# Row-blocked score matmuls in the exponential pass of a two-layer attention kernel

## The reference

```python
q, k, v = split_heads(x @ wq), split_heads(x @ wk), split_heads(x @ wv)   # 16 heads of 8
scores = jnp.einsum('bhqd,bhkd->bhqk', q, k)
scores = jnp.where(causal, scores, -jnp.inf)
attn = jax.nn.softmax(scores / np.sqrt(HEAD_DIM), axis=-1)
ctx = jnp.einsum('bhqk,bhkd->bhqd', attn, v)
```

## Time and profile before

| what | value |
|---|---|
| median of 3 runs | 1313.72 us (1313.71 to 1315.61) |
| span of the profiled execution | 1311.0 us |
| TensorE busy | 1194.1 us, 91% |
| VectorE busy | 1044.4 us, 80% |
| ScalarE busy | 723.5 us, 55% |
| mean granted TensorE clock | 0.975 of full speed |
| first attention layer, about | 200 to 643 us of the span |
| second attention layer, about | 846 to 1280 us of the span |

### The profile page before, as it was taken

One profiled execution on the slowest core, in us unless ns is written; L12 is line 12 of the kernel. 1 busy time (PEld: TensorE's weight loads), 2 busy tenths in 40 slices (PEclk: granted clock), 3 DMA queues, 4 the chain that ended last, 5 costly groups with the idle time before them and its releaser, 6 DMA issues.

```text
span 1311.0 us, 21446 instructions
## 1 busy us (share of the span) xinstructions
PE 1194.1 (91%) x7781; PEld 510.1 (39%) x7781; DVE 1044.4 (80%) x3015; ACT 723.5 (55%) x861; POOL 66.6 (5%) x64
## 2 busy tenths in 40 slices
PE   1999958999999999999699979599999999999997
PEld 1455533333333333334455537233333333333336
DVE  8976588999999887875447567799999989878764
ACT  1322115566777777777332224156667777777773
POOL 5111010000000000000101000100000000000000
PEclk9999979999999999999799989799999999999999
DMA  4100142000000000000000000510000000000001
GB/s 147 34 1 1 39 131 58 2 1 2 2 1 1 2 1 2 1 1 2 1 0 1 1 1 25 154 48 2 2 1 2 2 1 1 2 1 2 2 2 33
DMA packets 23510, 23.26 MB, mean 18 GB/s; under 512 B 3134, under 2 KB 21220, under 8 KB 23404
## 3 DMA queue, kind: packets, MB, share of 16 engines
q1 hardware_dynamic: 22252, 18.73, 4.9%
q0 software_dynamic: 1152, 3.15, 0.9%
HBM read 13.20 MB, written 8.39 MB: 16 GB/s over the span
## 4 chain that ended last, share of the span: by engine, by line
PE 70%; DVE 22%; issue 4%; ACT 2%; DMA 1%; SPq 0%; DVEq 0%; ACTq 0%
PE psum L1184 18%; PE psum L1204 17%; PE psum L1164 14%; PE psum L442 9%; DVE part_max L1314 8%; PE psum L466 2%; PE psum L903 2%; PE psum L1171 2%; DVE junk L1320 2%; DVE xn L167 1%; DVE norm_v L150 1%; PE psum L1224 1%; PE psum L918 1%; DVE norm_stats L141 1%; PE psum L427 1%
## 5 line engine op out<-in xcount | busy, mean ns | idle before, releaser
L1275 ACT ACTIVATE hidden<-psum,exp_scale 128x1024 f32<-128x1024 f32 (+3 forms) x640 | 597.7, 984 | 258.9 <-PE psum L1164 137.3
L1314 DVE TENSOR_REDUCE part_max<-psum 128x1 f32<-128x512 f32 x768 | 492.1, 686 | 59.1 <-PE psum L1204 53.9
L1204 PE MATMUL psum<-k_slots,q_slots 128*128 128x512 f16 (+3 forms) x1280 | 401.2, 356 | 34.2 <-DVE part_max L1314 12.2
L1164 PE MATMUL psum<-q_slots,k_slots 128*128 128x512 f16 (+3 forms) x1280 | 330.9, 348 | 6.3 <-ACT hidden L1275 3.5
L1184 PE MATMUL psum<-hidden,v_aug 128*9 128x512 f32 (+3 forms) x2560 | 293.7, 531 | 0.1
L1320 DVE CUSTOM_DVE_ANT_0 junk<-psum,causal_add 128x384 bf16<-128x384 f32 (+3 forms) x512 | 230.6, 488 | 49.0 <-PE psum L1204 45.9
L1204 PEld LDWEIGHTS psum<-k_slots,q_slots 128*128 128x128 f16 x1280 | 114.5, 97 | 361.1 <-DVE part_max L1314 177.5
L442 PE MATMUL psum<-parts,w_parts 128*128 128x512 f16 x768 | 180.4, 387 | 1.9 <-DVE parts L843 1.9
L1164 PEld LDWEIGHTS psum<-q_slots,k_slots 128*128 128x128 f16 x1280 | 118.3, 98 | 97.8 <-ACT hidden L1275 13.9
L442 PEld LDWEIGHTS psum<-parts,w_parts 128*128 128x128 f16 x768 | 73.7, 99 | 83.1 <-issue 6.8
L586 ACT CAST parts<-psum 128x512 f16<-128x512 f32 x64 | 37.2, 588 | 107.2 <-PE psum L427 107.2
(11 more groups left out here) (170 smaller groups left out, 730.5 us busy)
## 6 DMA issues: line engine op xcount, KB each, us to landing
q_slots<-q_rows SPq DMA_DIRECT2D x8, 512.0 KB, 3.7
k_slots<-k_rows POOLq DMA_DIRECT2D x24, 128.0 KB, 4.1
q_rows<-parts SPq DMA_DIRECT2D x18, 128.0 KB, 2.7
k_rows<-parts SPq DMA_DIRECT2D x18, 128.0 KB, 2.4
q_slots<-in_L_ffn_W_dram SPq DMA_DIRECT2D x2, 1024.0 KB, 6.5
k_slots<-k_rows SPq DMA_DIRECT2D x8, 128.0 KB, 3.9
q_slots<-nm_parts SPq DMA_DIRECT2D x64, 4.0 KB
out_dram<-x_res SPq DMA_DIRECT2D x4, 256.0 KB, 2.3
```

The lines of the kernel that those rows point to most:

```text
L1164: last = pe.matmul(psum[:, S_BANKS + 2 * (tile % 2) + par, off:CH], k_slots[:, G * g + 2 * pr + par, j * P:(j + 1) * P], q_slots[:, g, c * ...
L1204: last = pe.matmul(psum[:, bank, 0:w], q_slots[:, g, qb * P:(qb + 1) * P], k_slots[:, G * g + h, kc * CH:kc * CH + w], start=True, stop=True)
L1275: act.activation(probs[:, tile % NP, :, off:CH], psum[:, bank:bank + 2, off:CH], ACT.Exp, scale=exp_scale[:, layer:layer + 1]).then_inc(ex ...
L1314: dve.tensor_reduce(dst, psum[:, bank, :], axis=AX.X, op=ALU.max).then_inc(ring_read, 1)
```

## The change

The score matmuls of the exponential pass name the 32 partitions of their head in both operands, in place of all 128. A helper `rows_of(h)` gives the slice, and `load_k_rows` uses it for the same rows as before. The matmuls of the max pass keep their 128 rows. Columns, banks, waits and order stay as they are. The 96 partitions that are no longer read held zeros on the key side.

```diff
+            def rows_of(h):
+                return slice(SLOT * h, SLOT * (h + 1))
+
             def load_k_rows(engine, n, h):
                 cols = slice(n * CH, (n + 1) * CH)
-                return engine.dma_start(k_slots[SLOT * h:SLOT * (h + 1), h::G, cols],
+                return engine.dma_start(k_slots[rows_of(h), h::G, cols],
...
                     for par in range(2):
+                        rows = rows_of(2 * pr + par)
                         last = pe.matmul(psum[:, S_BANKS + 2 * (tile % 2) + par, off:CH],
-                                         k_slots[:, G * g + 2 * pr + par, j * P:(j + 1) * P],
-                                         q_slots[:, g, c * CH + off:(c + 1) * CH],
+                                         k_slots[rows, G * g + 2 * pr + par, j * P:(j + 1) * P],
+                                         q_slots[rows, g, c * CH + off:(c + 1) * CH],
                                          start=True, stop=q not in diagonal)
```

## The result

| kernel | median us | ratio to the kernel before, 95% interval |
|---|---|---|
| before | 1313.95 (1313.71 to 1315.61) | |
| changed | 1326.3 (1323.15 to 1328.65) | 1.009 (1.0078 to 1.0102) |

What follows compares the result with a forecast made beforehand. TensorE was taken to pace about 280 us of each attention layer, VectorE close behind. Stream: 115.1 - 117.7 + 12.8 = +10.2 us, +7 after gaps; 1311.0 + 7 + 2.7 = 1320.7, said as 1321 us, range 1300 to 1358.

Steps and rivals of the forecast that it cites:

- The clock: TensorE's granted clock in the attention layers: forecast to stay at 1.00, nothing in the sum; a fall had 5% chance.
- What it takes away: Exponential pass's score matmuls: the two of a pair run side by side, saving 117.7 us of TensorE's stream at best.
- Changes of layout: Ends of pairs, between whole array and row blocks: 1,212 further changes at 0.095 us each, adding 115.1 us.
- The second start: Within a pair, the second matmul starts 0.02 us behind the first: 12.8 us over 640 pairs (5.8 to 35.2).
- The lower row: Lower bound for a pair's second start: value matmuls of a group, 0.009 us apart, with weights of 9 columns.
- What is hidden: Attention layers' first stretch: changes falling into waits for VectorE cost nothing, half counted; +10.2 us of stream becomes +7.
- Rival 4: Attention layers: quarter-row matmuls with stops lower the clock to 1.2 GHz for a tenth of the time; +40, 1360; 5%.
- The readers' cap: Longest turns: VectorE's four max-pass reads take 2.74 of 2.81 us, so a turn could shorten by about 0.07 us.
- Rival 1: Ends of pairs: a layout change is cheaper, gaining below 0.087 us each; at 0.075 us, 1300 us; chance 18%.
- Rival 2: Within a pair, the second matmul's weights load in line: starts 0.055 us apart, +22 us, about 1343; chance 14%.
- rival 3: Pairs don't run side by side: starts 0.216 us apart, nothing saved, 115 us added, about 1410 us; chance 10%.
- The idle "issue": Sign of being right: idle time before first weight loads of exponential- and max-pass score matmuls, some 600 times a layer.

## Why the prediction came out as it did

The time lay in the range (1300 to 1358), and on the side with the larger chance. The result is +12 us, the forecast +7. The mechanism was right: pairs run side by side, and changes of layout eat up what this saves. That the work in the attention layers came so close to the forecast of 7 us (6.6 without the clock's share) is luck, as the terms below show: errors in the prices of +6, +3 and -11 us cancelled in good part. The clock, which stood at nothing in the sum, makes up most of the 5 us that were missing.

- **What it takes away.** 117.7 us of stream at best. The distance between the starts of a pair fell from 0.216 to 0.003 us, so nearly the whole slot is saved, as the step assumed; the kernel whose pairs share one block of rows puts its worth in time at 95 us.
- **Changes of layout.** Priced at 0.095 us from L452's 24 rows and the value block. Measured 0.100 at a pair, so 121 us for 1,212 in place of 115.1, 6 us more. The count was exact. Added to it, and not foreseen: the second mask matmul of a diagonal pair starts 0.067 us behind the first in place of 0.056, some 3 us over 256 pairs.
- **The second start.** This term was sized wrongly: 0.003 us and not 0.02, 2 us and not 12.8. The lower row, 0.009, was already too high by rounding; in nanoseconds the value matmuls start 0.007 us apart. The Trainium skill's at most 4 ns (TensorE: Matmul & The Clock Gate, "Why this matters for your kernels") was nearer than my estimate, and the trace agrees with it: 3 to 4 ns. In all, the work comes to 121 + 3 - 117.7 + 2 = +8 us against +10.2.
- **What is hidden.** I let half of the first six steps' +3.3 us a layer fall into gaps and counted 3.7 for the other ten steps. At the measured prices the work is 6.3 us for the first six steps of both layers and 1.9 for the rest. Measured: 5.1 in the first six; 1.5 in the rest without the clock's share (1.0 in nine steps, 0.5 in the last). So the waits hid little anywhere. One reason can be that the first six steps don't end with the first 120 us, as I took it: they last 149 us (200.4 to 349.4), and their last 30 lie where TensorE is busy throughout.
- **The clock.** I gave it 5% as a rival and nothing in the sum, and wrote that it stays at 1.00. It is a real part of the result: 4.6 of the 11.9 us in the profile, at a granted clock of 0.53 and 0.76 in the last steps, and full rows in the four shortest steps bring it back. Rival 4 was right that narrow matmuls can lower it; its place and size were wrong: I had written a tenth of the attention time. That it can be as large as that, and larger, shows in the kernels with both passes on 32 rows.
- **The readers' cap.** I multiplied VectorE's mean of 686 ns by four and concluded that a long turn can't fall below 2.74 us. This reading was wrong: records of VectorE overlap, and the same row has 492.1 us busy for 768 reads, 0.64 each. In the trace reads follow each other every 0.60 to 0.61 us, and turns of 2.46 and 2.47 us occurred. The forecast didn't need the cap, but it made a gain look smaller than it could be.
- **The rivals.** Rival 1 (a cheaper change) fails at 0.100 us, above its break-even of 0.087. The Trainium skill's rule that changing the tiling mode drains TensorE (TensorEngine Tiling, Key Properties) fits the 0.100 us at every pair. Rival 2 (0.055 us) and rival 3 (no side by side) fail at 0.003.
- **A sign that was off.** The idle "issue" was to appear some 600 times a layer before the loads of L1164 and L1204. The profile has it 332 and 216 times over both layers.
- **What I missed.** The forecast spoke of near cancellation and of the loss in the diagonals, but not of what follows from it: that leaving the diagonal out turns the sign.

What stays open: why the half off the diagonal gained 6.7 us where its work at the measured price says 11, and how much of the second layer's last step is the change's. There both kernels have one stretch of 3.4 us at half clock, at 1281.8 us before and 1282.9 after. Before, it came behind the last step, which had ended at 1277.4; after, it fell into it. In the first layer the half clock lasted 13.7 us where it had been 3.4.

## What to carry to other kernels

Narrowing a matmul to its block of rows buys nothing by itself. It buys one stream slot for each partner that can start beside it, and costs a fixed price at each end of the run of narrow matmuls (0.100 us here, nearly half of the 0.216 us that a 512-column matmul takes in the stream, and the same for 128 columns): count the ends, not the matmuls, and convert only runs whose partners save more than two ends cost. Four long partners in a run gained 24 us here with the order changed for it, two long ones 7 us, and short diagonal ones lost 19. And look at the granted clock after such a change, since narrow matmuls can cost more through it than they save.

## What the runs showed of the hardware that was not expected

- The granted clock can stay at 1.2 GHz with TensorE busy for 564.97 of 565 us, when its f16 score matmuls use 32 of 128 rows one at a time (mean 0.664 over the execution); later in the same execution it was full for 70 us with the same work. With up to four side by side the mean was 0.837, with only the max pass narrow 0.953, with only the exponential pass narrow 0.965, and 0.975 before.
- Two or four matmuls of 512 columns in different blocks of rows are all recorded within 0.39 us, with starts 0.003 to 0.004 us apart; a weight load of 32 x 128 is recorded as 91 ns, against 98 for 128 x 128.
- A change of layout costs about the same whichever way it goes and however wide the matmuls are: 0.098 us into row blocks and 0.101 out of them, 0.09 into the value block and 0.11 out of it, before and after.
- VectorE's maximum over 512 columns is recorded as 686 ns, but reads that follow each other start every 0.60 to 0.61 us.
